# The first attention of a two-layer kernel: the two maps are mixed by VectorE in one instruction behind the maxima, and GpSimd normalises the outputs

## The reference

```python
qkv = hidden_states @ Wqkv_w.T + Wqkv_b
p1 = attn_map(q[:, :, :, 0], k[:, :, :, 0])     # causal softmax of 1024 x 1024 scores, D = 128
p2 = attn_map(q[:, :, :, 1], k[:, :, :, 1])
p = p1 - lam * p2
o = jnp.einsum('bhqk,bkhe->bqhe', p, v)         # 256 columns a head
rms = jax.lax.rsqrt(jnp.mean(o * o, axis=-1, keepdims=True) + EPS)
o = o * rms * subln_w
o = o * (1.0 - LAMBDA_INIT)
return o @ out_w.T + out_b
```

## Time and profile before

| | |
|---|---|
| median of 3 runs | 1652.39 us (1649.94 to 1653.19) |
| the profiled execution | 1637.22 us, its span 1635.4 us |
| TensorE busy | 1526.0 us (93%), 10518 matmuls |
| VectorE busy | 1105.6 us (68%) |
| ScalarE busy | 938.1 us (57%) |
| GpSimd busy | 637.2 us (39%) |
| GpSimd's scaling of the second map, L2283 | 128 instructions, 97.6 us, mean 762 ns |
| GpSimd's sum of the maps, L2286 | 128 instructions, 182.8 us, mean 1428 ns |
| VectorE's `On`, L1724 | 104 instructions, 43.3 us, mean 459 ns |
| first attention | about 28 to 430 us and 820 to 1230 us of the span |

### The profile page before, as it was taken

The page is one execution under the profiler, slowest core; times in us unless marked ns, Lnnn a source line. Parts: engine busy times, 40 slices in busy tenths (PEclk is TensorE's granted clock), DMA queues, the critical chain, the costliest instruction groups (busy, mean ns, idle before and its releaser), DMA issues.

```text
span 1635.4 us, 30982 instructions
## 1 busy us (share of the span) xinstructions
PE 1526.0 (93%) x10518; PEld 1317.8 (81%) x10518; DVE 1105.6 (68%) x2963; ACT 938.1 (57%) x2054; POOL 637.2 (39%) x578
## 2 busy tenths in 40 slices
PE   8899999999999999999998999899999999998996
PEld 7888888888888677688987888888888886776885
DVE  7667767677745787574687676676767377884756
ACT  5666565665544577653656556556655346775453
POOL 2635444654561100243545445444654510031642
PEclk9999999999999999999999999999999999999998
DMA  3110000020120432124310100000202113322233
GB/s 133 46 53 17 27 1 16 26 90 3 40 70 10 71 56 52 30 108 142 110 73 14 65 17 27 17 4 22 92 1 57 52 32 63 59 65 81 68 133 111
DMA packets 48202, 88.08 MB, mean 54 GB/s; under 512 B 9600, under 2 KB 30480, under 8 KB 46928
## 3 DMA queue, kind: packets, MB, share of 16 engines
q1 hardware_dynamic: 43552, 75.28, 16.1%
q0 software_dynamic: 3744, 10.26, 1.8%
q10 hardware_dynamic: 768, 0.79, 0.2%
HBM read 60.18 MB, written 19.76 MB: 49 GB/s over the span
## 4 chain that ended last, share of the span: by engine, by line
PE 62%; DVE 15%; ACT 10%; issue 8%; POOL 4%; ACTq 1%; DMA 1%; DVEq 0%; POOLq 0%; SPq 0%
PE ps L410 15%; PE ps L412 14%; PE ps L411 14%; PE ps L1193 4%; PE ps L1210 4%; PE ps L1153 4%; ACT E L1407 4%; DVE E L1816 2%; PE ps L916 2%; POOL E L2286 2%; ACT PT_h L1389 1%; DVE On L1724 1%; PE ps L1189 1%; PE ps L846 1%; POOL xs L2397 1%
## 5 line engine op out<-in xcount | busy, mean ns | idle before, releaser
L1407 ACT ACTIVATE E<-E,nmax 128x128 f32<-128x128 f32 (+7 forms) x256 | 197.3, 772 | 211.6 <-DVE nmax L1816 211.1
L2283 POOL TENSOR_SCALAR E<-E,mixc 128x128 f32<-128x128 f32 (+7 forms) x128 | 97.6, 762 | 400.9 <-DVE mixc L1782 400.9
L1568 ACT ACTIVATE PT<-ps 128x512 f32<-128x512 f32 x288 | 154.9, 600 | 58.7 <-PE ps L1193 57.7
L2286 POOL TENSOR_TENSOR E<-E 128x128 f32<-128x128 f32 (+7 forms) x128 | 182.8, 1428 | 10.7
L410 PE MATMUL ps<-V_h,PT_h 128*128 128x256 f32 x576 | 164.7, 286 | 1.7 <-DVE O L1794 1.7
L412 PE MATMUL ps<-V_h,PT_l 128*128 128x256 f32 x576 | 162.7, 283 | 0.0
L411 PE MATMUL ps<-V_l,PT_h 128*128 128x256 f32 x576 | 162.7, 282 | 0.0
L410 PE MATMUL ps<-K_h,Q_h 128*128 128x512 f32 (+3 forms) x384 | 142.7, 372 | 6.3 <-DVE nmax L1816 2.9
L1789 DVE TENSOR_TENSOR PT_l<-ps,PT_h 128x128 fp32r<-128x128 f32 (+7 forms) x128 | 96.7, 755 | 63.2 <-ACT PT_h L1389 62.6
L2036 DVE CUSTOM_DVE_ANT_0 masked<-ps,causal 128x128 bf16<-128x128 f32 (+3 forms) x256 | 110.9, 487 | 39.7 <-PE ps L1153 38.0
L411 PE MATMUL ps<-K_l,Q_h 128*128 128x512 f32 (+3 forms) x384 | 133.8, 348 | 0.0
(11 more groups left out here) (267 smaller groups left out, 4579.1 us busy)
## 6 DMA issues: line engine op xcount, KB each, us to landing
Wa_raw<-in_wa SPq DMA_DIRECT2D x8, 1024.0 KB, 6.0
Fw_raw<-in_fa SPq DMA_DIRECT2D x32, 256.0 KB, 2.7
E_raw<-in_fe SPq DMA_DIRECT2D x8, 768.0 KB, 7.5
xs<-in_xs SPq DMA_DIRECT2D x2, 2967.0 KB, 12.0
Wo_raw<-in_wo SPq DMA_DIRECT2D x8, 512.0 KB, 3.6
yg<-ys SPq DMA_DIRECT2D x8, 512.0 KB, 5.7
xg<-xs SPq DMA_DIRECT2D x6, 645.0 KB, 7.8
KS<-QK_h SPq DMA_DIRECT2D x56, 64.0 KB
```

The costliest lines, as they stand in the source:

```text
L1407: nc.scalar.activation(e[:, 0:w], e[:, 0:w], ACT.Exp, scale=-1.0, bias=nmax[:, s % 4, m:m + 1], accum_out=lsum[:, s % 4, m:m + 1]).then_in ...
L1568: nc.scalar.activation(PT[:, at:at + HALF], bank1(RING1 + n % RING1), ACT.Exp, scale=SCALE1).then_inc(t_used, 1)
L2283: nc.gpsimd.tensor_scalar(e2, e2, mixc[:, n % 4:n % 4 + 1], 1.0, ALU.mult, ALU.mult).then_inc(mix_scaled, 1)
L2286: nc.gpsimd.tensor_tensor(e1, e1, e2, ALU.add).then_inc(p_ready, 1)
```

## The change

Three things, in the first attention only. VectorE does the whole mixing: behind `mixc` it makes `E1 = E2 * mixc + E1` in one instruction (scalar_tensor_tensor, all operands in SBUF) and signals `p_ready` itself. `mix(s-1)` moves from the head of VectorE's step s to behind the two maxima of s. And the `On` of groups 0 to 2 are made by GpSimd, as one product of 128x512 with the two heads' `orstd` columns spread over 256 columns each: tiles 0 and 1 at the head of the next group, behind a wait for the roots (`or_done`), tile 2 in step 7, tiles 3 and 4 in step 8, 5 and 6 in step 9, 7 in step 10 (`ON_STEPS`), each behind a wait for the transposes of tile t-2 (`ot_ps`) and ahead of that step's `Wa_l`. GpSimd's two mixing instructions are gone. VectorE keeps tiles 0 and 1 of the last groups' tail. GpSimd's former `out_normalise`, for the rest of the last groups, is only renamed.

```diff
+ON_STEPS = {7: (2,), 8: (3, 4), 9: (5, 6), 10: (7,)}
...
         def out_normalise(it, g, t):
 
-            if t >= 2:
-                dve.wait_ge(ot_ps, NT * it + t - 1)
             for h in range(2):
...
                     if kind == "t":
                         out_low(it - 1, t)
-                        if 1 <= t < NT - 1:
-                            out_normalise(it - 1, g + 1, t + 1)
...
                                                op1=ALU.mult).then_inc(mix_ready, 1)
+                w = (q_tile(n, last) + 1) * P
+                e1, e2 = E1[n % 2][:, 0:w], E2[n % 2][:, 0:w]
+                dve.wait_ge(mix_ready, STEPS0 * it + n + 1)
+                nc.vector.scalar_tensor_tensor(out=e1, in0=e2, scalar=mixc[:, n % 4:n % 4 + 1], in1=e1, op0=ALU.mult,
+                                               op1=ALU.add).then_inc(p_ready, 1)
...
             for s in range(STEPS0):
-                if s >= 1:
-                    mix(s - 1)
-                if out and s in (2, 3):
-                    if s == 2 and last:
+                if out and s == 2:
+                    if last:
                         dve.wait_ge(xb_done, 2 * b + 1)
-                    elif s == 2:
+                    else:
                         dve.wait_ge(xd_in, 16 * b + 16)
-                    out_normalise(it - 1, g + 1, s - 2)
                 if s >= 2:
                     low(s - 2)
...
+                if s >= 1:
+                    mix(s - 1)
                 for t in v_tiles(s):
...
+        def out_normalise(it, g, t):
+
+            if t >= 2:
+                pool.wait_ge(ot_ps, NT * it + t - 1)
+                pool.nop(nofuse=True)
+            scales = orstd[:].rearrange("p (h t) -> p h t", h=2)[:, :, t:t + 1].to_broadcast([P, 2, E0])
+            nc.gpsimd.tensor_tensor(On[t % 2][:], O[:, t, bass.ds(g % 2 * 2, 2), :], scales, ALU.mult).then_inc(on_done, 1)
+
+        def attn0_group(b, g, out, last):
             it = b * GROUPS0 + g
+            if out:
+                pool.wait_ge(or_done, 2 * it)
+                pool.nop(nofuse=True)
+                for t in range(2):
+                    out_normalise(it - 1, g + 1, t)
             for n in range(STEPS0):
-                w = (q_tile(n, last) + 1) * P
-                e1, e2 = E1[n % 2][:, 0:w], E2[n % 2][:, 0:w]
-                pool.wait_ge(mix_ready, STEPS0 * it + n + 1)
-                pool.nop(nofuse=True)
-                nc.gpsimd.tensor_scalar(e2, e2, mixc[:, n % 4:n % 4 + 1], 1.0, ALU.mult,
-                                        ALU.mult).then_inc(mix_scaled, 1)
-                pool.wait_ge(mix_scaled, STEPS0 * it + n + 1)
-                nc.gpsimd.tensor_tensor(e1, e1, e2, ALU.add).then_inc(p_ready, 1)
                 for t in v_tiles(n):
...
+                for t in ON_STEPS.get(n, ()) if out else ():
+                    out_normalise(it - 1, g + 1, t)
                 if n in SPLIT_STEPS:
```

14 lines of the change are left out of this document (7 added, 7 removed).

## The result

The changed kernel takes 1730.3 us (median; 1728.1 to 1736.4), the kernel before beside it 1652.3 us. The ratio is 1.048 (95% interval 1.0449 to 1.0512): 78 us slower, where 53 were forecast (1705, range 1686 to 1732). Its profiled execution took 1728.15 us, its span is 1726.3 us.

A forecast was written before the change was run, and what follows sets the result against it. TensorE, busy 93% of the span, was taken as the bound, so only its waits count. Eight groups x 6.7 + 4 x 0.6 - 2 x 1.5 = +53 us on 1652.4: 1705 us, range 1686 to 1732.

The forecast's parts named there:

- the round of step 7: Reciprocal, mix, transposes, PT_h, low and two maxima of step 7 would follow in one row: 6.47 us, 5.54 before.
- not the sum of VectorE's work: Claim that the mix's place in VectorE's queue, behind the maxima, decides the loss, rather than VectorE's total work.
- its upper end: Range's end at 1732 us, 27 above forecast: clock 14, and either uncovered mixes in four groups 12 or a third of collisions.
- steps 4 to 7: Four rounds of a group, 4.27 to 6.47 us each, would take 21.5 us instead of 19.2: +2.3 us.
- steps 8 to 12, with collisions: Longer rounds covered by TensorE's output products, costed at nothing; mixes meeting GpSimd's work add 0.6 us per middle group.
- steps 13 to 15: Three rounds, as wide as those of steps 5 to 7, would take 17.2 us instead of 14.8: +2.4 us.
- transposes of tile 14, to the next group: They would start 1.70 us behind the last maximum's end instead of 0.34 us before it: +2.0 us.
- Steps 0 to 3 costed at nothing: At the start of a group the longer row was taken as covered by TensorE's output products: 0 us.
- The rounds on a straight line between steps 3 and 7: Rounds between 3.54 us in step 3 and 6.47 us in step 7 would lie on a line, 0.73 us apart.
- the clock rival: TensorE's clock falls in the new waits before wide transposes, once a group: 14 us more, 1719 us; chance 0.10.
- GpSimd is free there after the change: 0 to 2.0 us less, I take 1.5: In the last groups' tail, VectorE's first two On would no longer stand behind GpSimd's instructions: 1.5 us less each.
- the rival's 36 us: Mixes in steps 0 to 2 and 8 to 11 all meet GpSimd, uncovered: 36 us more, 1740 us; chance 0.10.

The follow-up runs named there:

- e1: The changed kernel with VectorE's one-instruction mix moved back to the head of the step, ahead of low and the two maxima: ratio 1.0191 to the kernel before.
- e9: e1 with GpSimd holding the V_l of a step until that step's mix is done: ratio 1.0047 to the kernel before.
- e3: The changed kernel with the On of groups 0 to 2 back on VectorE at their old places: 1736.5 us, ratio 1.0506 to the kernel before.
- e10: e9 with the On of groups 0 to 2 back on VectorE: ratio 1.0208 to the kernel before.
- e7: The changed kernel with ScalarE rounding the V tiles (V_h) a step later, behind PT_h: ratio 1.0445 to the kernel before.
- e6: The changed kernel with GpSimd holding back Wo_l of the last groups until VectorE has made On of tiles 0 and 1: ratio 1.0428 to the kernel before.
- e2: The kernel before, still mixing on GpSimd, with only the On of groups 0 to 2 moved to GpSimd: ratio 1.0187 to the kernel before.

## Why the prediction was right, and where it was short

**The mechanism held.** Each term of the round of step 7 is in the rows after: 0.45 (278.39 to 278.84) as forecast, the mix 1.02 (0.98), the hand-over 0.14 (0.15), transposes 0.85 (0.82), PT_h 0.80 (0.78), low and maxima 3.28 (3.23), and twice 0.03 between. Counted from the end of the maximum's row, 0.07 us behind the reciprocal's start, that is 6.53, forecast 6.47. That the place decides is shown by e1 and e9: the same instructions, with the mix at the head of the step and without the collision, take 1.0047. Its "not the sum of VectorE's work" holds for the changed kernel (e3: 48 more On cost some 6 us) but not at the head of the step (e10: the same On cost 26 us). Of the signs that it named, the waits for the mix (112.0 us, 1.34 in step 7) and the 6.5 us between the maxima came as told; a middle group took 115.5 to 115.9 us for 113 to 115, the mix of 1024 columns 1.28 us for 1.2, and TensorE's waits for `On` were gone except in the last groups' tails.

**The sum was short by 23 us** (eight groups longer by 75.6 us in the two profiled executions, 53 forecast; by the medians 78). The time lies inside the range by 2 us only, and partly by luck: its upper end was made of a falling clock, uncovered mixes in steps 8 to 11 and collisions of the mix, and most of the 23 us came from elsewhere. (The reasons given for its lower end add up to 17 us, not 19, those for its upper end to 26, not 27.) The terms, for a middle group of the first half:

| term | forecast | measured |
|---|---|---|
| steps 0 to 3 | 0 | +0.5 |
| steps 4 to 7 | +2.3 | +3.4 |
| steps 8 to 12, with collisions | +0.6 | +0.6 |
| steps 13 to 15 | +2.4 | +2.6 |
| transposes of tile 14, to the next group | +2.0 | +2.0 |
| together | +7.3 | +9.2 |

- *Steps 8 to 12* came out as forecast and for the reason given. One mix in each middle group meets an On, that of 1024 columns, and takes 0.71 us too long; the round behind it takes 6.56 us, and 6.02 in e3, where nothing is met. The rest of these steps nets to nothing, since the shorter round of step 10 (5.84 for 6.41), with VectorE's On gone, pays for the others. That the sizes agree is partly luck: the sum expected 1.9 meetings, half of them covered, and one of the six On that it puts in these steps belongs to step 7.
- *"Steps 0 to 3 costed at nothing"* was wrong by 0.5 us; e7 takes 0.44 of them back, so most of it was V_h in ScalarE's queue. The prediction named what is queued behind `low`, but not that the mix was also moved past the bias of V.
- *The rounds on a straight line between steps 3 and 7.* Steps 13, 14 and 15, which have no V tile beside them, took 5.11, 5.84 and 6.49 for 5.00, 5.74 and 6.47: the line was good to 0.1. Steps 4, 5 and 6 took 4.63, 5.34 and 6.10 for 4.27, 5.00 and 5.74. Of these 1.1 us, 0.2 is V_h (e7). In step 4 the row through TensorE's scores is seen in the timeline (0.20 us). In step 6 the transposes wait for the bias of the last V tile (9.6 us in 8 waits); how much of its 0.36 us is that wasn't tested.
- *The first groups*, forecast at 6.7, became 10.5 and 10.7 us longer, though the range expected them shorter. Here VectorE has the sums and splits of another matrix between mix and low. And the clock rival came true in part: TensorE waited 2.04 us before five transposes, and the window behind it shows the granted clock at its lower level, 1.2 of 2.4 GHz; the round of that step took 7.37 us, where e6, with the clock whole there, took 5.85. Each of the two first groups has two such stretches, the same groups of before one each. In e7, which has none in them, they are 7.4 and 8.0 us longer than before's, so most of the miss went with the clock and V_h; how much is whose wasn't tested.

```profile
94.25 0.83 PE L916 MATMUL ps<-ident_r,E 128*128 128x128 f32 x5 [2.04 <-DVE E L1784]
...
96.00:98.00 2.00, 2.00 (x7) 1.72 (x7) 1.20 (x2) 0.00 (x0) 0.00 (x0) 0.50 0.00 0
```

- *The last groups* were the largest miss: +5.2 each forecast, +11.8 and +10.4 measured. "GpSimd is free there after the change: 0 to 2.0 us less, I take 1.5" was the term that failed. It took the instructions of GpSimd that make the 3.29 us of the earlier trace rows for the mixing, which goes. It was Wo_l, which the change doesn't remove: the mixing had ended at 421.78, before the On began, and GpSimd then stood idle for 1.28 us waiting for ScalarE's Wo_h, as it does after the change. What the change moved is the moment: VectorE's On and ScalarE's Wo_h now come together, and Wo_l blocks the first tile instead of the second. Why just there wasn't looked into. e6 shows the size, 3.5 and 2.2 us (the 1.3 between them went with the clock): with Wo_l out of the way the last groups are 8.3 us longer than before, and of the 3 us that are still missing 1 each is in steps 4 to 7 and 13 to 15.
- *Collisions.* The 128 mixes took 111.1 us. At their undisturbed lengths (0.35, 0.48, 0.62, 0.75, 0.89, 1.02, 1.15 and 1.28 us) they would take 104.7, so 6.4 us were lost, in twelve mixes: eight of 128 columns that meet a V_l (0.43 us each) and four of 1024 that meet an On (0.71 each). The sum had 4 x 1.2 us and counted half of it, 2.4; the rival's 36 us are far off. The collision that cost more, On with Wo_l in the tail, it didn't name. VectorE's mix and GpSimd's On in the changed kernel:

```profile
293.19 1.99 DVE L1784 SCALAR_TENSOR_TENSOR E<-E,mixc 128x1024 f32<-128x1024 f32 x1
...
293.06 1.04 POOL L2282 TENSOR_TENSOR On<-O,orstd 128x512 f32<-128x512 f32 x1 [3.62 <-PE ps L846]
```

- *On on GpSimd at nothing* held: TensorE never waits for it outside the tail, it took 1.04 us instead of 1.29, and by e3 it brings some 6 us. It held only because the mix left GpSimd's queue, which e2 shows and the prediction didn't say.
